# Attention of layer four: third batch's adds and normalising in one piece, stream's maxima begun four slots later

## What is computed

```python
x = x + jnp.tanh(g_ffn[2]) * _L2_ffn_ref(_layernorm(x, axis=-1), ...)      # experts of layer three
x = x + jnp.tanh(g_xattn[3]) * _L3_xattn_ref(_layernorm(x, axis=-1), ctx_512, ctx_512)

def _L3_xattn_ref(q, k, v):
    B, S, E = (2, 256, 256)
    QH, KVH = (32, 8)
    D = E // QH
    qh = q.reshape(b, s, KVH, G, D).transpose(0, 2, 3, 1, 4)
    kh = k.reshape(b, s, KVH, D).transpose(0, 2, 1, 3)
    vh = v.reshape(b, s, KVH, D).transpose(0, 2, 1, 3)
    scores = jnp.einsum('bkgsd,bktd->bkgst', qh, kh) * scale
    attn = jax.nn.softmax(scores, axis=-1)
    out = jnp.einsum('bkgst,bktd->bkgsd', attn, vh)
```

## Time and profile before

| | |
|---|---|
| median of 3 runs | 818.59 |
| lowest and highest | 817.67, 820.45 |
| span of the profiled execution | 816.7 |
| mean granted clock of PE | 0.945 |
| PE busy | 707.3 (87% of the span) |
| DVE busy | 539.1 (66%) |
| ACT busy | 353.9 (43%) |
| POOL busy | 214.8 (26%) |

### The profile page before, as it was taken

The page is one execution under the profiler, slowest core; times in us unless marked ns, Lnnn a source line. Parts: engine busy times, 40 slices in busy tenths (PEclk is TensorE's granted clock), DMA queues, the critical chain, the costliest instruction groups (busy, mean ns, idle before and its releaser), DMA issues. The chain is left out here.

```text
span 816.7 us, 14003 instructions
## 1 busy us (share of the span) xinstructions
PE 707.3 (87%) x4479; PEld 467.5 (57%) x4485; DVE 539.1 (66%) x1627; ACT 353.9 (43%) x622; POOL 214.8 (26%) x307
## 2 busy tenths in 40 slices
PE   9999997988987785798868988986888899999995
PEld 4644466666764674576746767652233227776773
DVE  5786898788773879678861571657876756423554
ACT  2663455455445664221124314334488693212220
POOL 0002595002000132013313550632252220242340
PEclk9999999999998999789998999997599999999998
DMA  6994421040000310000160150011000043032315
GB/s 197 342 218 102 145 75 46 4 156 1 3 2 0 104 53 1 1 1 26 40 214 33 54 192 14 34 40 66 2 2 2 3 150 65 33 110 79 105 61 171
DMA packets 55566, 60.24 MB, mean 74 GB/s; under 512 B 13847, under 2 KB 48808, under 8 KB 55496
## 3 DMA queue, kind: packets, MB, share of 16 engines
q1 hardware_dynamic: 50408, 46.02, 19.6%
q0 software_dynamic: 4848, 13.28, 4.7%
q10 hardware_dynamic: 240, 0.05, 0.0%
HBM read 34.92 MB, written 24.20 MB: 72 GB/s over the span
## 5 line engine op out<-in xcount | busy, mean ns | idle before, releaser
L1928 ACT ACTIVATE arenas<-psum 128x512 f32<-128x512 f32 (+6 forms) x89 | 63.2, 732 | 60.3 <-PE psum L1134 51.6
L3156 DVE TENSOR_REDUCE arenas<-psum 128x2 f32<-128x512 f32 x96 | 62.0, 685 | 19.6 <-PE psum L1706 18.5
L943 POOL TENSOR_SCALAR arenas<-arenas,small 128x1024 f32<-128x1024 f32 x8 | 9.0, 1128 | 161.2 <-DVE small L2895 161.2
L960 POOL DMA_INDIRECT experts_l<-shared,small x30 | 29.1, 969 | 81.4 <-ACT shared L2228 72.8
L1123 PE MATMUL psum<-conb 128*128 128x512 bf16 x167 | 44.6, 413 | 4.9 <-ACT early L1928 3.1
L1134 PE MATMUL psum<-conb,shared 128*128 128x128 bf16 (+2 forms) x512 | 39.2, 231 | 10.3 <-issue 5.7
L1134 PE MATMUL psum<-con,early 128*128 128x128 f32 (+1 forms) x188 | 33.3, 287 | 15.5 <-ACT late L1928 4.4
L1134 PEld LDWEIGHTS psum<-conb,shared 128*128 128x128 bf16 (+2 forms) x512 | 34.0, 118 | 17.8 <-issue 14.9
L3121 DVE TENSOR_TENSOR shared<-shared,psum 128x128 f32<-128x128 f32 x30 | 8.6, 287 | 53.3 <-PE psum L1659 26.6
L1928 ACT ACTIVATE late<-psum 128x512 f32<-128x512 f32 (+1 forms) x51 | 25.6, 501 | 40.3 <-PE psum L1134 40.3
L2275 ACT ACTIVATE early<-psum 128x1024 f32<-128x1024 f32 x32 | 32.4, 1037 | 22.3 <-PE psum L1723 22.0
(11 more groups left out here) (436 smaller groups left out, 1792.2 us busy)
## 6 DMA issues: line engine op xcount, KB each, us to landing
sorted_l<-late SPq DMA_DIRECT2D x3, 1920.0 KB, 16.7
early<-sorted_l SPq DMA_DIRECT2D x6, 645.0 KB, 5.7
early<-in_L_ffn_sw SPq DMA_DIRECT2D x3, 1024.0 KB, 9.2
late<-sorted_l SPq DMA_DIRECT2D x23, 129.0 KB, 2.1
sorted_l<-late SPq DMA_DIRECT2D x1, 2944.0 KB, 23.5
early<-in_L_ffn_We_gate_up SPq DMA_DIRECT2D x2, 1408.0 KB
early<-in_L_ffn_expert_w SPq DMA_DIRECT2D x2, 1024.0 KB, 6.6
early<-in_L_ffn_w SPq DMA_DIRECT2D x1, 2048.0 KB, 8.2
```

What stands on the lines that cost most here:

```text
L960: pool.indirect_dma_start(expert_rows2[p], bass.IndirectOffsetOnAxis(dest2[p][:, i:i + 1], 0), out_r2[k], None).then_inc(outs_sent[k], 16)
L1928: act.activation(dst, view(v), ACT.Copy, scale=scale).then_inc(f.drained(i, key), 1)
L3156: dve.tensor_reduce(nm, q3d(f.slot(0, ("max", w, k)), 2, S), X, ALU.max, negate=True)\
```

## The change

Two things are changed. DVE takes the whole of batch 2's adds and normalising in one piece (`alone`) ahead of the first maximum of unit 2. PE issues no maximum in slots 0 to 3, three in each of slots 4 to 11, and two from slot 12 on. After slot 11 both kernels have issued 24 maxima.

```diff
         SHIFT_AT = 3
+        LATE_MAX = 4
...
                     exp3(w, m)
-                    next(maxima, None)
+                    for _ in range(0 if g < LATE_MAX else 2 if g < 3 * LATE_MAX else 1):
+                        next(maxima, None)
                     for at, key in inserts3[w]:
                         if at == m:
                             turn_columns3(*key)
                     if g >= 3 and g % 2 == 1:
                         pair = (g - 3) // 2
                         values3(pair // 4, pair % 4)
-                    next(maxima, None)
+                    if g >= LATE_MAX:
+                        next(maxima, None)
                     if m == 4 and w > 0:
                         tokens3(w - 1)
...
             def attention3():
                 for w in range(2, UNITS):
                     beside = routed_back(1, [w], xn3_rows(w)) if w < 4 else steps(0)
+                    if w == 2:
+                        alone(beside)
                     for k in range(16):
                         maximum3(w, k)
```

## The result

| | before | changed |
|---|---|---|
| median of 19 runs | 818.59 | 821.76 |
| lowest and highest | 816.0, 824.34 | 819.67, 827.66 |
| span of the profiled execution | 816.7 | 819.1 |

The ratio of the changed kernel to the one before is 1.004, with a 95% interval from 1.0021 to 1.006. That is 3.2 us more by the medians, where 5.5 were forecast.

What follows compares the result with a forecast made beforehand. Bound by a loop of maximum matmul, DVE reduce and bank release at half clock. Terms 0.1 - 0.60 + 4.14 + 1.88 gave 5.5 us, taking 818.59 to 824.1; range 819.3 to 827.5, the forecast's own 822.5 to 826.

Steps and rivals of the forecast that it cites:

- the third term: Slots 10 and 11: batch 3's first adds lose the cover of PE's values and cost 1.88 us.
- The piece of batch 2: Slots 0 to 4: DVE's piece takes 5.97 us, so the values of slot 5 start 0.1 us later.
- The lost steps of batch 2: Second pair of before: without batch 2's interleaved steps it falls from 4.98 to 4.38, 0.60 us gained.
- six maxima at 0.69: Slots 6 to 11: six owed maxima, two in each pair, cost one reduce of 0.69 us each, 4.14 in all.
- rival 2: Slots 6 to 11: extra maxima fit into DVE's idle time and cost 0; time 818.1 to 820.0; chance 0.12.
- Batch 3's uncovered adds: Slots 10 and 11: the first adds, no longer covered by PE's values, delay slot 11's values by 1.88 us.
- two maxima, +1.38: Pair ending at slot 11's values: its two owed maxima add 1.38 us, part of the 4.14 for all six.
- The clock, taken as neutral: From slot 12: full clock returns 2.7 us after the transposes begin, as before; one pair later or sooner shifts 1.3 us.
- Rival 1: Slots 4 to 11: denser slots bring PE's clock back early; time 818.5 to 821.1; chance 0.20.
- The sign that was written for it: In the changed stretch: a granted clock of 1.00 before 590 would show the prediction wrong.
- Rival 3: Clock returns later still (825.4), or six maxima cost matmul and reduce, 1.33 each, 8.0 in all (827.9); chance 0.08.
- the rival of the experiments: Whole stretch: the loss is only longer time at half clock, so both kernels with held clock are level at 814.3.

Runs made afterwards that it cites:

- The second comparison: Changed kernel unchanged, 6 runs on another occasion against the kernel before: ratio 1.0077, 5.5 us more by the medians.
- e1: Kernel before with only batch 2's piece on DVE, maxima still two a slot from slot 0: 831.34 against 827.57, ratio 1.0044.
- e3: Changed kernel with batch 3's steps begun behind unit 3's first maximum instead of its third: 832.07 against 827.57 for the kernel before, ratio 1.0058.
- e7: Changed kernel with both pairs of batch 3's adds behind unit 3's first maximum: 823.65 against 818.32 for the kernel before, ratio 1.0077.
- the second profiles: Profiles of both kernels run again unchanged: before 817.31, changed 823.79, each against 818.32.
- e6: Changed kernel once more, unchanged, against the kernel before: 823.79 against 818.32, ratio 1.0077.
- e8: Kernel before with unread matmuls filling PE's waits ahead of the stretch and in slots 0 to 11: 814.33 against 818.32, ratio 0.9946.
- e11: e8 repeated, against the kernel before: 815.40 against 818.91, ratio 0.9956.
- e9: Changed kernel with e8's fillers and 16 more in slot 4: 820.01 against 818.91 for the kernel before, ratio 1.0017.
- e4: Kernel before with fillers ahead of the stretch and in slots 0 to 7 only: 827.94 against 827.57, ratio 0.9998.
- e10: e8 with both pairs of batch 3's adds behind unit 3's third maximum: 817.73 against 818.91 for the kernel before, ratio 0.9976.

## Why the prediction was right

The direction was right, and 821.76 lies within the stated 819.3 to 827.5. It lies under the forecast's own range of 822.5 to 826, though: 3.2 us were measured where 5.5 were written. The second comparison came nearer (5.5 us). Slot 11's values stood at 593.65 where 593.7 was written, but that close a match is luck. The first score itself came 0.3 us later than before, and counted from it they were 5.17 us late, where the sum gives 5.5. Two rows of DVE's timeline of before, behind those of the earlier trace rows, are needed for the third term:

```profile
585.43 1.37 DVE L3141 SCALAR_TENSOR_TENSOR xs<-arenas,dispatch,xs 128x256 f32<-128x256 f32 x2
586.87 0.69 DVE L3156 TENSOR_REDUCE arenas<-psum 128x2 f32<-128x512 f32 x1
```

By the prediction's own terms:

- **The piece of batch 2, +0.1.** Its sum of 5.97 measured 5.89 (564.55 to 570.44). The values of slot 5 were 0.2 late. Right.
- **The lost steps of batch 2, -0.60, and six maxima at 0.69.** The pairs took 5.77 and 5.78. Against the undisturbed 4.38 of the earlier trace rows a further maximum costs 0.70. Right, and shown: the idle 1.70 in front of each six reduces is rival 2's, and it stayed unused. e1 adds that the loss needs no dense slots, since without them PE waits in one place (8.66 us) for the same piece of DVE's.
- **Batch 3's uncovered adds, +1.88, with two maxima, +1.38.** Here the sum was too large. The third pair grew by 8.99 - 6.20 = 2.79, where these two terms give 3.26. The first adds came out as written: they lay open for 2.00 us (588.38 to 590.38). What came out smaller stands around them. The two further reduces ahead of them took 1.21 (587.17 to 588.38). From the reduce behind them to the next one it was 1.99 (590.38 to 592.37), where it was 2.31 before (584.56 to 586.87), mostly because the second pair of adds took 1.11 instead of 1.37. The sum had no term for that. The last 0.1 is that the adds of before were not quite covered: the reduce behind them starts 2.60 us after the values there, and 2.51 where no adds stand ahead of it. e3 and e7 agree with the mechanism, once the statistic that moved up with the adds is counted.
- **The clock, taken as neutral.** The sum assumed its return 2.7 us after slot 12's transposes began. It returned 0.5 us after (596.49 to 597.0), and 0.6 us was given back from slot 11 to 13; between the second profiles it was 1.4. So the sum's 5.5 us were not carried to the end. The stretch is 4.6 us longer than before by the first profiles, 3.9 by the second ones.
- **The end.** 4.6 us in the stretch and 3.2 in the median: between them stands the clock, in this stretch (1.0 us between two profiles of the kernel before) and at the routed tiles (2.5 us between the two first profiles). The loss of the stretch, 3.9 to 4.6 us, lies between the two comparisons, 3.2 and 5.5. How much of the difference is chance and how much the changed kernel's phase against the clock was not settled.

**The rivals.** Rival 1, that the denser slots wake the clock, did not happen in either profile of the changed kernel: it was 0.50 from slot 4's third maximum to the end of slot 11 in both. The sign that was written for it, a clock of 1.00 before 590, did appear in e6, from 566.0 to 569.8. But it came at slot 4's first two maxima, and nearly all of it fell into PE's wait, so nothing came sooner by it. The rule of the Trainium skill (TensorE: Matmul & The Clock Gate, "Part 1: The HAM clock gate"), that activity releases the throttled state, agrees with the fillers, at which the clock was 1.00 in e8 and e11; the denser slots stayed at 0.50 with PE 82% busy. Rival 2 fell with the pairs of 5.8. Rival 3's price for matmul and reduce, 1.33 a maximum, was twice the measured one. That the loss is only the half clock, the rival of the experiments, fell with e9: about 3.9 us of it are there with the clock held but for 3.4 us.

## What to carry to other kernels

When one engine feeds another through two banks, work that is done in a wait is nearly free, and the same work outside it is not. Here DVE's three reduces during the DMA's landing cost nothing, and batch 2's steps between reduces cost 0.26 and 0.60 us in two pairs (4.64 and 4.98 against 4.38). The same steps in one piece made PE wait 4.1 us and left six maxima owed, which cost 0.6 to 0.7 us each. Count what the stream owes at the first point where both orders agree again, and price it at the slower engine's duration. Before moving work around in a stretch, look at its granted clock: matmuls in PE's waits gave 3.5 and 4.0 us here in the two runs with twelve filled slots, and nothing in the one with eight. And when steps are moved up, look at which step moves up behind them: in e3 and e7 it was a statistic, and it took 0.3 us of a gain of 0.8 to 1.0.

## What was not expected of the hardware

- Fillers of 512 columns, three in each slot (0.82 us of PE), kept the granted clock at 1.00 through a stretch that ran at 0.50 for 34 us. Between e4, on another chip, and e8 the edits differ by four more filled slots only, and in e4 it fell for 6.8 us. In e9 and e10, with twelve filled slots, it still fell for 3.4 and 3.2 us after PE had waited 2.29 and 2.50 us.
- The clock of before changed from run to run in the same place: back 33.0 us after the first score in one profile and 36.2 in the other.
- Twice the clock in the first 33 us of this stretch shortened it by 3.6 us only (114.4 to 110.8). DVE's reduces of 0.69 us take as long at either level; the fillers' own time is in the 110.8, and no run tells the two apart.
- A pair of adds with the same operands took 0.86 to 2.01 us in these runs. It was 0.92 in e3 as the first pair, at 595.03, and 1.74 as the second, at 597.43; POOL began to split batch 2's rows at 595.79. The Trainium skill (SBUF — State Buffer, section "SBUF: two separate sides") describes such a lock between the two engines. These times fit it, but no run here took POOL's part away to show it.
